# Softmax row sums of a transformer block: joining more key chunks into one running sum on GpSimd, and a new order of the setup's score maxima

## The reference

```python
mod = silu(condition) @ Wada + bada                # shift, scale, gate for attention and for the MLP
xm = layernorm(x, g1, be1) * (1.0 + sc_a[:, None, :]) + sh_a[:, None, :]
q, k, v = split_heads(xm @ Wqkv)
scores = where(causal, q @ k.T * hd ** -0.5, -inf)
x = x + gt_a * ((softmax(scores) @ v) @ Wproj + bproj)
xm = layernorm(x, g2, be2) * (1.0 + sc_m[:, None, :]) + sh_m[:, None, :]
x = x + gt_m * (gelu(xm @ W1 + b1) @ W2 + b2)
```

## Time and profile before

| | us |
|---|---|
| median of 3 runs (lowest, highest) | 3178.81 (3177.39, 3179.57) |
| the profiled execution's own time | 3182.6 |
| span of its trace | 3180.8 |
| busy: PE / DVE / POOL / ACT | 3128.7 / 2344.8 / 1745.5 / 1195.9 |

### The profile page before, as it was taken

One profiled execution on the slowest core, in us unless ns is written; L12 is line 12 of the kernel. 1 busy time (PEld: TensorE's weight loads), 2 busy tenths in 40 slices (PEclk: granted clock), 3 DMA queues, 4 the chain that ended last, 5 costly groups with the idle time before them and its releaser, 6 DMA issues.

```text
span 3180.8 us, 68318 instructions
## 1 busy us (share of the span) xinstructions
PE 3128.7 (98%) x24936; PEld 2523.5 (79%) x24936; DVE 2344.8 (74%) x2981; ACT 1195.9 (38%) x2354; POOL 1745.5 (55%) x1385
## 2 busy tenths in 40 slices
PE   8999999999999999999999999999999999999999
PEld 5677777777777777766688888989888898988888
DVE  4678887887888787766876767777676777767773
ACT  3355555555555555566421211212111121211211
POOL 3288888888888888888743323333232333333232
PEclk9999999999999999999999999999999999999999
DMA  6666566666656665666612223122221313222120
GB/s 241 216 180 192 175 188 185 177 184 187 195 170 192 186 180 165 199 195 169 160 55 66 67 51 79 40 79 56 63 72 46 79 40 79 56 63 76 42 66 14
DMA packets 304611, 391.85 MB, mean 123 GB/s; under 512 B 24280, under 2 KB 206072, under 8 KB 304432
## 3 DMA queue, kind: packets, MB, share of 16 engines
q1 hardware_dynamic: 292320, 371.86, 41.1%
q10 hardware_dynamic: 12112, 17.42, 1.6%
HBM read 270.66 MB, written 118.00 MB: 122 GB/s over the span
## 4 chain that ended last, share of the span: by engine, by line
PE 89%; DVE 6%; issue 2%; DMA 1%; ACT 1%; SPq 1%; POOL 0%; DVEq 0%; ACTq 0%; POOLq 0%
PE psH L1014 22%; PE psY L1027 22%; PE psA L786 9%; PE psT L840 9%; PE psA L878 8%; PE psP L915 5%; PE psA L790 5%; PE psS L809 4%; DVE mx L1350 2%; PE psA L851 2%; PE psA L758 1%; DVE psS L1346 1%; PE psA L900 1%; PE psA L895 1%; DMA oin<-sums 1%
## 5 line engine op out<-in xcount | busy, mean ns | idle before, releaser
L1611 POOL TENSOR_TENSOR h_l<-h_full,h_h 128x256 fp32r<-128x256 f32 x512 | 488.8, 955 | 1079.1 <-DVE h_h L1523 1079.1
L1350 DVE TENSOR_REDUCE mx<-psS 128x4 f32<-128x2048 f32 (+3 forms) x384 | 665.9, 1756 | 126.1 <-PE psS L809 88.4
L1102 ACT ACTIVATE e<-psT 128x512 f32<-128x512 f32 (+1 forms) x1202 | 605.4, 555 | 374.0 <-PE psT L840 369.9
L1225 ACT ACTIVATE h_full<-psH,b1c 128x256 f32<-128x256 f32 x512 | 242.5, 474 | 1220.6 <-PE psH L1014 1220.6
L1014 PE MATMUL psH<-a_l,w1p_h 128*128 128x256 f32 x2048 | 577.5, 282 | 0.0
L1014 PE MATMUL psH<-a_h,w1p_l 128*128 128x256 f32 x2048 | 577.3, 282 | 0.0
L1014 PE MATMUL psH<-a_h,w1p_h 128*128 128x256 f32 x2048 | 575.4, 281 | 0.0
L1669 POOL TENSOR_TENSOR es<-e 128x512 f32<-128x512 f32 (+1 forms) x242 | 446.1, 1844 | 164.0 <-ACT e L1102 80.0
L1523 DVE CAST h_h<-h_full 128x256 fp32r<-128x256 f32 x512 | 179.8, 352 | 402.7 <-ACT h_full L1225 400.0
L840 PEld LDWEIGHTS psT<-qst,kst 97*128 97x128 f32 x2404 | 349.3, 190 | 113.3 <-issue 70.6
L840 PE MATMUL psT<-qst,kst 97*128 97x256 f32 (+1 forms) x2404 | 410.8, 290 | 3.3 <-ACT e L1102 2.1
(11 more groups left out here) (118 smaller groups left out, 5216.6 us busy)
## 6 DMA issues: line engine op xcount, KB each, us to landing
qk_split<-qk_hl SPq DMA_DIRECT2D x128, 512.0 KB, 3.5
kst<-qk_split SPq DMA_DIRECT2D x128, 256.0 KB, 3.8
qst<-qk_split SPq DMA_DIRECT2D x128, 256.0 KB, 4.1
xin<-in_x_dram SPq DMA_DIRECT2D x64, 256.0 KB, 3.4
values<-vout ACTq DMA_DIRECT2D x64, 256.0 KB, 2.3
kmx<-qk_split SPq DMA_DIRECT2D x32, 512.0 KB, 4.6
qmx<-qk_split SPq DMA_DIRECT2D x32, 512.0 KB, 5.7
kst<-qk_split SPq DMA_DIRECT2D x128, 128.0 KB, 3.8
```

Of the source, the lines that this page charges most:

```text
L1102: act.activation(e[:, s % ERING, 2 * hp:2 * hp + 2, 0:w], score_bank(s, hp, with_a)[:, :, 0:w], ACT.Exp, scale=SCALE).then_inc(sem("exp_do ...
L1225: act.activation(h_full[:, m % 4, :], psH[:, m % 4, 0:RA], ACT.Gelu, bias=b1c[:, m:m + 1])\
L1350: reduce = dve.tensor_reduce(mx[:, part, :, qt], psS[:, :, col:col + w], AX_X, ALU.max)
L1611: return pool.tensor_tensor(dst, full, high.bitcast(F32), ALU.subtract)
```

## The change

In a body's second head group slot 6 joins the place of slots 4 and 5, and slot 8 that of slot 7, in the 13 bodies `with_a`. POOL adds the whole first chunk of such a slot with `half_add`, after both masks, and the second chunk's 128 columns with `add`; PE then takes one set of 4 products of 256 columns from the place, and the sets of slots 5 and 7 (L851) are gone. In the setup, the pieces 5 to 8 of the first maxima and 1 and 2 of the second stand at other items, and the first body scores step 0 before the first six matrix products of its item.

```diff
-MAX_ALONE_AT = {(1, 5): (0, 0), (1, 6): (0, 1), (1, 7): (0, 2), (1, 8): (0, 3), (1, 9): (0, 4), (1, 10): (0, 5),
-                (2, 0): (0, 6), (2, 1): (0, 7), (2, 3): (0, 8), (2, 6): (1, 0), (2, 8): (1, 1), (2, 10): (1, 2)}
-TURN_ALONE_AT, PLACE_ALONE_AT = (2, 5), (2, 7)
+MAX_ALONE_AT = {(1, 5): (0, 0), (1, 6): (0, 1), (1, 7): (0, 2), (1, 8): (0, 3), (1, 9): (0, 4), (2, 0): (0, 5),
+                (2, 1): (0, 6), (2, 3): (0, 7), (2, 4): (0, 8), (2, 7): (1, 0), (2, 8): (1, 1), (2, 9): (1, 2)}
+TURN_ALONE_AT, PLACE_ALONE_AT = (2, 6), (2, 8)
...
-SUM_GROUPS = {True: [(0, 1, 2), (3,), (4, 5)] + [(i,) for i in range(6, SLOTS)], False: [(i,) for i in range(SLOTS)]}
+SUM_GROUPS = {(True, 0): [(0, 1, 2), (3,), (4, 5)] + ALONE[6:], (True, 1): [(0, 1, 2), (3,), (4, 5, 6), (7, 8), (9,)],
+              (False, 0): ALONE, (False, 1): ALONE}
...
-                    ahead = u == 0 and s == 0
-                    if ahead:
-                        a_item(AHEAD, *item_at(0), False, with_ln)
...
-                    if at and not late and not ahead:
+                    if at and not late:
                         a_item(u + AHEAD, *at, False, with_ln)
...
                 if i != slots[0]:
                     if i in DIAG_SLOTS:
-                        pool.wait_ge(sem("masked"), (u * 2 + h) * len(DIAG) + 2 * DIAG_SLOTS.index(i) + 1)
+                        pool.wait_ge(sem("masked"), (u * 2 + h) * len(DIAG) + 2 * DIAG_SLOTS.index(i) + 2)
...
                     mask(u, s)
-                    if s % 2 == 0:
+                    if (s % 2 == 1) == (s // 2 % SLOTS in DIAG_SLOTS):
                         half_add(u, s // 2, with_a)
-                    else:
+                    if s % 2 == 1:
                         add(u, s // 2, with_a)
```

More of the change, by code:

```diff
@@ L146 @@
 OTHER_SLOTS = [i for i in range(SLOTS) if i not in DIAG_SLOTS]
-SUM_GROUPS = {True: [(0, 1, 2), (3,), (4, 5)] + [(i,) for i in range(6, SLOTS)], False: [(i,) for i in range(SLOTS)]}
-HALF_ADDED = [i for g in SUM_GROUPS[True] for i in g[1:]]
-HALF_ADDS = len(HALF_ADDED)
+ALONE = [(i,) for i in range(SLOTS)]
+SUM_GROUPS = {(True, 0): [(0, 1, 2), (3,), (4, 5)] + ALONE[6:], (True, 1): [(0, 1, 2), (3,), (4, 5, 6), (7, 8), (9,)],
+              (False, 0): ALONE, (False, 1): ALONE}
+HALF_ADDED = [(h, i) for h in range(2) for g in SUM_GROUPS[True, h] for i in g[1:]]
 def sum_place(h, i, with_a):
-    groups = SUM_GROUPS[with_a]
+    groups = SUM_GROUPS[with_a, h]
     n = next(n for n, g in enumerate(groups) if i in g)
     last = groups[n - SRING][-1]
-    return (h * len(groups) + n) % SRING, groups[n], last if n >= SRING else last - SLOTS
-SUMS_END = {with_a: [g[-1] for g in groups] for with_a, groups in SUM_GROUPS.items()}
-assert all({groups[-2][-1], groups[-1][-1]} <= set(DIAG_SLOTS) and groups[-1] == (9,) for groups in SUM_GROUPS.values())
+    return (h * len(SUM_GROUPS[with_a, 0]) + n) % SRING, groups[n], last if n >= SRING else last - SLOTS
+SUMS_END = {key: [g[-1] for g in groups] for key, groups in SUM_GROUPS.items()}
+assert all(ends[-2:] == [8, 9] and {8, 9} <= set(DIAG_SLOTS) for ends in SUMS_END.values())
+assert all((len(SUM_GROUPS[a, 0]) + len(SUM_GROUPS[a, 1])) % SRING == 0 for a in (True, False))
 LAST_SLOT = {CHUNKS[2 * i][0]: i for i in DIAG_SLOTS}
@@ L933, in body @@
                         piece = None
-                    sums = slot and s // 2 >= 2 and (s // 2 - 2) % SLOTS in [i for i in SUMS_END[with_a] if i not in DIAG_SLOTS]
+                    sums = slot and s // 2 >= 2 and (s // 2 - 2) % SLOTS in [i for i in SUMS_END[with_a, (s // 2 - 2) // SLOTS] if i not in DIAG_SLOTS]
                     scores(u, s, 0, with_a)
@@ L1658, in add @@
                 if i != slots[0]:
-                    pool.wait_ge(sem("half_added"), (u * 2 + h) * HALF_ADDS + HALF_ADDED.index(i) + 1)
+                    pool.wait_ge(sem("half_added"), u * len(HALF_ADDED) + HALF_ADDED.index((h, i)) + 1)
                     if i in DIAG_SLOTS:
```

## The result

The changed kernel takes 3229.11 us (median of 6 runs, 3226.43 to 3232.73), the kernel before 3178.95 (6 runs): a ratio of 1.0159, 95% interval [1.0149, 1.0169]. That is 50 us slower; the forecast was 37 slower, 3216, with a range of 3189 to 3243.

The account below looks back on a forecast made before the run. PE sets the pace, busy 91.5 of a body's 92.1 us. Twelve bodies at +3.35 (+40), the 13th -0.3 and setup -2.7 gave +37 on 3178.8: 3216 us, own range 3206 to 3228, 8-in-10 range 3189 to 3243.

Parts of the forecast that it names:

- PE's 0.92 per body saved: On PE, the product sets of slots 5 and 7 go, 0.46 us each: a gain of 0.92 per body.
- slot 6's add meets no DVE work: On POOL, slot 6's new add meets no DVE work and PE asks for its sum several us later: costs nothing.
- Slot 8's sum 0.37 late: A DVE CAST delays POOL's small add after slot 8's whole add, so PE starts at 427.68, not 427.31: loss 0.37 us.
- DVE's splits late: On DVE, splits k = 1 and 2 end late; step 39's reduction ends at 432.1, not 430.2, and PE waits at step 1.
- Split k = 3 against slot 0's add: DVE's CAST is issued at the same moment as POOL's add; PE's L809 of step 3 comes some 3.8 us late.
- +3.35 per body: Net loss per body: 3.8 us of lateness at step 3 less slot 5's 0.46; the period becomes 95.4 instead of 92.1.
- Setup -2.7: In setup, once: earlier splits, neighbouring pieces and the first body's order together save 2.7 us, between 0 and 4.
- From there on every engine stands as before relative to PE: After PE's late L809 of step 3 in a body, nothing further is lost beyond the 3.8 us.
- POOL goes first twice: Rival: slot 1's whole add shuts out DVE's TENSOR_TENSOR a second time; 5.5 us per body, 3242 us; chance 0.12.
- Only the first lateness: Rival: split k = 3 slips ahead of slot 0's add; +1.35 us per body, 3192 us; chance 0.11.

Follow-up runs that it names:

- Slot 6 alone: The whole change, but slots 7 and 8 apart again and only slot 6 joined, against the kernel before: 3173.64 us, ratio 0.9978.
- the splits out of the way: The changed kernel with splits k = 1, 2 and 3 left out in the blocks that the bodies form, against the kernel before: 3168.88 us, ratio 0.9970.
- the filler: The changed kernel, with PE repeating products of the next step's scores while it waits at steps 1 and 3, against the kernel before: 3214.82 us, ratio 1.0111.
- the earlier add: The changed kernel, with POOL's whole adds of slots 6 and 8 moved between the slot's two masks, against the kernel before: 3182.65 us, ratio 1.0013.
- the one other order of DVE's queue: The changed kernel, with the maxima's piece of step 39 ahead of split k = 2 on DVE, against the kernel before: 3229.91 us, ratio 1.0163.
- slot 8 alone: The change with slots 7 and 8 joined and slot 6 apart from 4 and 5, against the kernel before: 3223.21 us, ratio 1.0139.

## Why the prediction was right, and where it was short

- *PE's 0.92 per body saved*: it is there. Slot 6 alone shows 0.40 of its 0.46 in the period of a body, and with the splits out of the way a body is 0.67 shorter, where 0.92 less 0.37 gives 0.55. That slot 6's add meets no DVE work was put down without a row, since it stands 10 us ahead of slot 8's, outside the rows read; the run with slot 6 alone bears it out.
- *Slot 8's sum 0.37 late*: PE's L902 starts at 432.74, about 0.3 after L880's share of 0.65 from 431.78. Right.
- *DVE's splits late*: forecast 1.36 and 1.64 us for the CAST and the TENSOR_TENSOR of k = 1, found 1.28 and 1.66; the wait at step 1 forecast 1.3 or 1.4, found 1.30.
- *Split k = 3 against slot 0's add*: forecast at the same moment, with one of the two near 3 us, found 0.02 us apart and 2.75; the wait at step 3 forecast about 2.5, found 2.10.
- *+3.35 per body*: forecast a period of 95.4, found 95.1 to 95.7 (mean 95.4) where the clock stayed up, and 95.3 to 95.6 with the filler. The kernel with the filler takes 3214.8 where the sum gave 3216.
- *Setup -2.7*: found -2.9 in the trace.
- *Missing*: the sum priced PE's waits at their length and nothing after them. The step that failed is "From there on every engine stands as before relative to PE". The clock falls around the end of the wait of step 3, in 8 of the bodies of the trace of after: five short falls at 1.0 us and three long ones at 2.0 each, some 11 us. The filler puts the whole term at 14 us; the other 3 were not traced. 36 (3214.8 less 3179.1) and 14 make the 50.

The mechanism was right, and the size in part luck: 3229.11 lies above the forecast's own 3206 to 3228, and inside the range to 3243 only because that took in the rival "POOL goes first twice", whose mechanism did not occur: slot 1's add starts at 440.85, behind the TENSOR_TENSOR's end at 440.27. The clock, which no part of the forecast priced, made up the difference. "Only the first lateness" did not happen either. Of the places in a body where PE's two waits could come from, the experiments leave one: the moment of slot 8's add.

The best complete version found is slot 6 joined in the second group with the new setup, 3173.64 us: 0.22% [0.13%, 0.31%] faster than before. Slot 8's saving was had neither by the earlier add nor by the one other order of DVE's queue; further orders were not tried.

## What to carry to other kernels

Between VectorE and GpSimd, count not only how busy each is but which instruction of the one stands in flight when the other issues: two adds of 2.4 us on GpSimd, with 16 us free per body, made a body 3.3 us longer at one moment and 0.4 when slot 8's stood 0.6 us earlier, both with PE's saving taken off. Follow a held instruction down its own queue to the first thing that TensorE waits for, and look there for the slack; here it was 0.6 us at one place and 0.05 at the next. And a wait of TensorE can cost more than its length: look at the granted clock at its end and behind it.

## What had not been expected of the hardware

The granted clock fell to 1.2 GHz around the end of PE's idle 2.1 us at step 3 (with another 1.3 us idle some 6 us before), between 0.5 us ahead of that end and 0.9 us behind it, but not in every body: 4 of the 12 with the same two waits kept 2.4 GHz, and 9 of 12 did with slot 8 alone. Where it fell it stayed low for about 3.5 us, as from 444.6 to 448.1, or for about twice that. One wait was enough: with slot 6 in both head groups it fell in 12 of 13 bodies, at the end of the single wait of 2.4 us or up to 1.7 us behind it. In the kernel before, it fell in no body but the last, at about 1557.8, after a wait of 1.76 us and during one of 1.17. With the filler, whose 12 bodies have a longest idle time of 0.84 us, three of them of 1.15, none fell. With split k = 3 left out, where the longest is 1.3, none of the first 13 did. Why it falls in some bodies and not in others was not settled.
